# A fused graph network kernel: three pieces of the graph loaded and squared earlier, and the statistics of the sums moved behind the second kind's n term

## What is computed

```python
x = _layernorm(x + _L0_gnn_ref(x, adj, adj, gat_W, gat_a, edge_*, node_*), axis=-1)
x = _layernorm(x + _L1_gnn_ref(x, adj, adj, W_proj, b_proj, W_gcn, b_gcn), axis=-1)

# layer 0
node_support = node_adj_norm @ h
edge_output = _gru_cell(node_support, h, edge_Wih, edge_Whh, ...)
edge_support = mean over 3 heads of (softmax attention over adj * adj) @ (h @ W)
node_output = _gru_cell(edge_support, h, node_Wih, node_Whh, ...)
return de[:, None] * edge_output + dn[:, None] * node_output

# a cell
r = sigmoid(ir + hr); z = sigmoid(iz + hz); n = tanh(inn + r * hn)
return (1.0 - z) * n + z * hstate

# layer 1
filt = tanh(adj * adj) * (adj > 0)          # then the 350 largest of a row are kept
h2 = tanh(h @ W_proj + b_proj)
feat = relu(new_adj @ (h2 @ W_gcn) + b_gcn)
```

## Time and profile before

| what | value |
|---|---|
| median of 3 runs | 1315.2 us (1315.08 to 1315.21) |
| profiled execution, its own time | 1315.81 us |
| its span | 1314.5 us |
| TensorE clock granted | 0.999 of full |
| busy: PE / DVE / ACT / POOL | 1302.3 / 1015.3 / 936.2 / 100.6 us |
| transfers | 231.17 MB, 176 GB/s over the span |

### The profile page before, as it was taken

How to read it: one execution, slowest core, us unless ns; L and a number is a source line. 1 busy time by engine, 2 the same in 40 slices (tenths; PEclk the granted TensorE clock), 3 DMA queues, 4 the chain that set the end, 5 groups by cost and what they waited for, 6 DMA issues and landing times.

```text
span 1314.5 us, 12241 instructions
## 1 busy us (share of the span) xinstructions
PE 1302.3 (99%) x4197; PEld 588.7 (45%) x4197; DVE 1015.3 (77%) x1420; ACT 936.2 (71%) x968; POOL 100.6 (8%) x194
## 2 busy tenths in 40 slices
PE   9999999999999999999999999999999999999998
PEld 4444444444444444444444444444444444444445
DVE  3243333457998998999989989899857888788886
ACT  5545555348988889889889898898945556555563
POOL 0100001000100100100100100100101662000000
PEclk9999999999999999999999999999999999999999
DMA  9978888254242242242433323222114458888870
GB/s 372 414 262 274 294 296 291 84 211 145 88 146 103 97 144 96 97 144 97 149 112 108 144 96 139 102 96 96 64 34 163 146 175 290 301 289 298 294 266 18
DMA packets 45191, 231.17 MB, mean 176 GB/s; under 512 B 6530, under 2 KB 12610, under 8 KB 19778
## 3 DMA queue, kind: packets, MB, share of 16 engines
q1 hardware_dynamic: 42416, 227.50, 49.1%
q10 hardware_dynamic: 2706, 2.82, 0.6%
HBM read 226.01 MB, written 4.29 MB: 175 GB/s over the span
## 4 chain that ended last, share of the span: by engine, by line
PE 92%; DVE 5%; issue 1%; DMA 1%; ACT 1%; SPq 0%; DVEq 0%
PE t_y_ps L1888 49%; PE ns_ps L455 17%; PE t_y_ps L1438 13%; PE rows_ps L1438 4%; PE t_y_ps L1866 3%; PE t_es_ps L1855 1%; PE pos_ps L469 1%; PE t_y_ps L1403 1%; PE t_y_ps L1405 1%; DVE pieces L1249 1%; PE t_y_ps L1457 1%; ACT pieces L1166 1%; DMA mask<-in_adj_c 1%; DVE pieces L1244 1%; DVE pieces L1268 0%
## 5 line engine op out<-in xcount | busy, mean ns | idle before, releaser
L1888 PE MATMUL t_y_ps<-mask,x_sb 128*128 128x512 f32 x1536 | 662.6, 592 | 0.2 <-DVE mask L1804 0.2
L1888 PEld LDWEIGHTS t_y_ps<-mask,x_sb 128*128 128x128 f32 x1536 | 290.6, 190 | 365.3 <-issue 349.5
L1804 DVE TENSOR_TENSOR mask<-mask 128x1536 f32<-128x1536 f32 x256 | 449.4, 1756 | 0.7 <-ACT mask L1686 0.7
L1686 ACT ACTIVATE mask<-mask,ones 128x1536 f32<-128x1536 f32 x256 | 399.7, 1562 | 0.0
L1679 ACT ACTIVATE mask<-mask,pieces 128x512 f32<-128x512 f32 x352 | 241.4, 712 | 35.1 <-PE t_y_ps L1888 32.8
L1790 DVE TENSOR_SCALAR mask<-mask,e_cols 128x512 f32<-128x512 f32 x416 | 188.5, 485 | 50.1 <-PE t_y_ps L1888 44.0
L455 PE MATMUL ns_ps<-pieces,x_sb 128*128 128x512 f32 x504 | 225.1, 601 | 0.6 <-DMA x_sb<-in_x_p 0.6
L1191 ACT ACTIVATE mask<-mask 128x2048 f32<-128x2048 f32 x64 | 122.4, 1912 | 82.6 <-DVE mask L1314 82.6
L1438 PE MATMUL t_y_ps<-mask 128*128 128x512 f32 (+1 forms) x448 | 173.8, 547 | 1.5 <-DVE pieces L1249 1.5
L314 DVE TENSOR_SCALAR mask<-pieces 128x2048 fp8e4<-128x2048 f32 x64 | 77.0, 1224 | 90.1 <-DMA pieces<-in_adj_c 74.2
L1314 DVE SCALAR_TENSOR_TENSOR mask<-mask 128x2048 f32<-128x2048 f32 x64 | 143.0, 2281 | 4.3 <-DMA mask<-in_adj_c 4.3
(11 more groups left out here) (186 smaller groups left out, 575.4 us busy)
## 6 DMA issues: line engine op xcount, KB each, us to landing
mask<-in_adj_c SPq DMA_DIRECT2D x128, 1024.0 KB, 4.8
pieces<-in_adj_c SPq DMA_DIRECT2D x62, 1024.0 KB, 5.1
mask<-scratch_shifts SPq DMA_DIRECT2D x8, 1536.0 KB, 7.9
pieces<-in_adj_c SPq DMA_DIRECT2D x8, 256.0 KB, 5.0
mask<-in_x_t SPq DMA_DIRECT2D x8, 256.0 KB, 10.5
pieces<-in_x_t SPq DMA_DIRECT2D x8, 256.0 KB, 2.9
pieces<-scratch_ns_t SPq DMA_DIRECT2D x8, 256.0 KB, 4.2
mask<-in_diag SPq DMA_DIRECT2D x8, 256.0 KB, 5.6
```

Of the source, the lines that this page charges most:

```text
L1686: nc.scalar.activation(t, t, ACT.Exp, bias=ones[:, :], scale=-1.0).then_inc(exped, 1)
L1804: nc.vector.tensor_tensor(term(n), term(n), a, ALU.mult).then_inc(terms, 1)
L1888: mm = nc.tensor.matmul(y_ps[c % 2][h][:, :], x_sb[:, k, :], term(n)[:, h, :], start=k == 0, stop=k == NB - 1)
```

## The change

What it does:

- The loads of the graph's pieces 0 to 2 are issued by SP during the last chunk of attention, each as soon as the last term or shift that lay in its place has been used.
- Square and tanh of piece 0 run at the end of attention, ahead of the last `scale_y` and of the gate loop. The squares of pieces 1 and 2 are in step 0 of the gate loop, ahead of and behind `pre_n("edge")`; their tanh in steps 0 and 1.
- `measure_y` stands behind `pre_n("node")` and not ahead of it.
- SP loads x and ns for a step once the gates two steps earlier are read and x is weighed, and not once `cells` is up.
- The first graph products wait each for the one reader of their own bank.

```diff
@@ sync_tail
-        for u in range(READY):
-            load_unit(u)
         for c in range(2, NCHUNK):
+            sp.wait_ge(gates_read["node"], 3 * (c - 1))
+            sp.wait_ge(mix_step, 3 * (c - 1))
+            load_in(sp, c)
             sp.wait_ge(cells, c - 1)
-            load_in(sp, c)
             load_diag(sp, c)
-            load_unit(READY + c - 2)
+            load_unit(sp, READY + c - 2)
@@ scalar_tail
+        tanh(act, 0)
         for c in range(NCHUNK):
...
-            if c - 1 in FILTERED_IN:
-                tanh(FILTERED_IN[c - 1])
+            if c < 2:
+                tanh(act, c + 1)
             make_n("edge", c)
@@ vector_tail
         for c in range(NCHUNK):
+            if c == 0:
+                square_a(dve, 1)
             pre_n("edge", c)
+            if c == 0:
+                square_a(dve, 2)
             weigh_n("edge", c)
-            if c and c in FILTERED_IN:
-                square_a(FILTERED_IN[c])
             weigh_x(c)
+            pre_n("node", c)
             if c:
                 measure_y(c - 1)
-            pre_n("node", c)
             weigh_n("node", c)
             make_y(c)
@@ graph
-            if g == 0 and c == 0:
-                pe.wait_ge(gates_read["node"], 3 * NCHUNK)
-                pe.wait_ge(pre_step["node"], 2 * NCHUNK)
+            if g == 0 and c < len(f_ps):
+                if GATES[c] == "in_n":
+                    pe.wait_ge(pre_step["node"], 2 * NCHUNK)
+                else:
+                    pe.wait_ge(gates_read["node"], 3 * NCHUNK - 2 + READS.index(GATES[c]))
@@ sync_program
             for c in range(2):
                 load_in(sp, c)
+            sp.wait_ge(y_scaled, HEADS * (NCHUNK - 1))
+            sp.wait_ge(gaps_act, NB * (NCHUNK - 1))
+            for u in range(READY):
+                last = max((n for n in range(NPIECES) if piece_at(n) < (u + 1) * PW and u * PW < piece_at(n) + PW), default=-1)
+                if last >= 0:
+                    sp.wait_ge(terms, PIECE * (last + 1))
+                load_unit(sp, u)
@@ vector_program
+            square_a(dve, 0)
             scale_y(NCHUNK - 1)
             vector_tail(dve)
```

More of the change, by code:

```diff
@@ L985 @@
 READY = 3
-FILTERED_IN = {0: 0, 1: 1, 4: 2}
 W_SLOT, IN_SLOT = 3, 4
@@ L1077, in load_in, with load_unit, square_a, tanh @@
         sp.dma_start(ns_t[c % 2], dram["ns_t"][:, c * CW:(c + 1) * CW]).then_inc(in_loaded[c % 2], 16)
+    def load_unit(sp, u):
+        c, g = divmod(u, NPIECE)
+        sp.dma_start(piece(u).rearrange("p (k n) -> p k n", n=CW), dram["adj_c"][c, :, g * PIECE:(g + 1) * PIECE, :]
+                     ).then_inc(loaded[u % G_RING], 16)
+    def square_a(dve, u):
+        dve.wait_ge(loaded[u % G_RING], 16 * (u // G_RING + 1))
+        nc.vector.scalar_tensor_tensor(piece(u), piece(u), 0.0, piece(u), ALU.max, ALU.mult).then_inc(squared_a, 1)
+    def tanh(act, u):
+        act.wait_ge(squared_a, u + 1)
+        nc.scalar.activation(piece(u), piece(u), ACT.Tanh).then_inc(filtered, 1)
     def make_biases(dve):
@@ L1187, in make_h2 @@
             nc.scalar.activation(g_all[:, rows(c), :].rearrange("p r f -> p (r f)"), pre_h[c % 2], ACT.Tanh).then_inc(copied, 1)
-        def tanh(u):
-            act.wait_ge(squared_a, u + 1)
-            nc.scalar.activation(piece(u), piece(u), ACT.Tanh).then_inc(filtered, 1)
         def take_out(i):
@@ L1223, in scalar_tail @@
         copy_rows(end)
-        tanh(3)
+        tanh(act, 3)
         make_h2(end - 1)
         for u in range(4, NPIECE - 1):
-            tanh(u)
+            tanh(act, u)
         make_h2(end)
-        tanh(NPIECE - 1)
+        tanh(act, NPIECE - 1)
         for u in range(NPIECE, NPIECES):
-            tanh(u)
+            tanh(act, u)
             c, g = divmod(u, NPIECE)
@@ L1244, in pre_n @@
             nc.vector.scalar_tensor_tensor(hid_n[k], r[k], 1.0, hid_n[k], ALU.add, ALU.mult).then_inc(pre_step[k], 1)
-            if c == 0 and k == "edge":
-                square_a(FILTERED_IN[0])
             dve.wait_ge(pre_step[k], 2 * c + 1)
@@ L1310, in finish_x @@
             normalize(rows(c), moments, root, x_done)
-        def square_a(u):
-            dve.wait_ge(loaded[u % G_RING], 16 * (u // G_RING + 1))
-            nc.vector.scalar_tensor_tensor(piece(u), piece(u), 0.0, piece(u), ALU.max, ALU.mult).then_inc(squared_a, 1)
         def add_x1(i):
@@ L1366, in vector_tail @@
         end = NCHUNK - 1
-        square_a(3)
+        square_a(dve, 3)
         scale_h(end - 1)
-        square_a(4)
+        square_a(dve, 4)
         measure_y(end)
-        square_a(5)
-        square_a(6)
+        square_a(dve, 5)
+        square_a(dve, 6)
         scale_h(end)
-        square_a(7)
+        square_a(dve, 7)
         for u in range(NPIECE, NPIECES):
-            square_a(u)
+            square_a(dve, u)
             c, g = divmod(u, NPIECE)
@@ L1502, in tensor_tail @@
         feed(last)
-    return load_weights, load_in, load_diag, make_biases, center_weights, keep_center, sync_tail, pool_tail, scalar_tail, vector_tail, tensor_tail
+    return load_weights, load_in, load_diag, load_unit, square_a, make_biases, center_weights, keep_center, sync_tail, pool_tail, scalar_tail, vector_tail, tensor_tail
 def on_dve(k):
@@ L1587, in heads_of @@
             return slice(STRIPS * g % HEADS, STRIPS * g % HEADS + STRIPS)
-        (load_weights, load_in, load_diag, make_biases, center_weights, keep_center, sync_tail, pool_tail, scalar_tail, vector_tail,
+        (load_weights, load_in, load_diag, load_unit, square_a, make_biases, center_weights, keep_center, sync_tail, pool_tail, scalar_tail, vector_tail,
          tensor_tail) = tail_programs(
```

## The result

| | before | changed |
|---|---|---|
| median | 1315.24 us (1315.08 to 1315.8, 6 runs) | 1320.94 us (1319.67 to 1322.12, 6 runs) |
| profiled execution, its time | 1315.81 us | 1320.76 us |
| its span | 1314.5 us | 1319.4 us |
| first product of the gate loop | 978.41 | 979.09 |
| first product of the graph's piece 7 | 1104.8 (worked out in the prediction) | 1109.69 |

The ratio is 1.0042, 95% interval 1.0029 to 1.0055: slower by 5.7 us where 4.1 were forecast.

The account below looks back on a forecast made before the run. TensorE was taken as the bound, waiting about 6.5 us; the change closes a 12.9 us loop against its 11.63 us step, delaying graph piece 7 by 4.1 us: 1315.8 + 4.1 = 1319.9, median 1319.3 us, range 1313.3 to 1321.0.

Parts of the forecast that it names:

- The saved waits: TensorE's waits from attention's last product to the graph's first: removing all of them gives at most 6.5 us.
- the three waits of the earlier trace: TensorE waits 0.96 us before 991.55, 0.32 before 1005.47 and 1.46 before 1079.42; the change was to remove them.
- 5.7 forecast: Square 0 on DVE at the end of attention, ahead of the gate loop: it has 5.7 us to spare.
- the 0.32 us: TensorE's wait for a transfer before 1005.47: loading x and ns one wait earlier takes it away.
- The chain on GpSimd: GpSimd's 15 small root instructions, nine held by DVE instead of six: 8.1 us, not 6.7.
- The loop: Gate loop: statistics, GpSimd's roots, ACT's scaling and read, DVE's next statistics take 12.9 us; TensorE needs 11.63.
- The one choice that the prediction named: GpSimd's bias addition lies on DVE's L1244 by only 0.7 us; without the collision the loop is 12.4 us.
- Statistics of chunk 6: DVE's gate loop: after six turns of 12.9 us they end at 1082.9; before it was 1077.8.
- over 2 us for tanh 4 and again for tanh 7: Graph stage, a sign in the profile: TensorE waits over 2 us for each of these two tanh.
- the forecast itself: Whole kernel: a loop of 12.6 to 13.1 us gives 1317.5 to 1320.5 us, chance 0.62.
- a longer loop: Rival: ACT's or DVE's hand-overs cost 0.05 us more at each of eight; loop 13.3, 1321.7 us; 0.07 including late loads.
- +4.1 us: Graph stage: piece 7 can start at 1108.9 instead of 1104.8, and the stage moves as a whole by 4.1 us.

Follow-up runs that it names:

- The parts that give: Changed kernel with statistics ahead again and the old SP order and TensorE waits, leaving only the early loads, squares and tanh: 1310.82 us, ratio 0.9963.
- opened at ACT: Changed kernel, statistics still late, with ACT's scaling moved behind its read of r for the second kind: 1312.32 us, ratio 0.9978.
- the bias addition's collision: Changed kernel with GpSimd adding the bias to one column of each row only, the rest left out: 1316.71 us, ratio 1.0011.
- the late statistics and piece 7 ahead: Changed kernel, statistics still late, with square and tanh of piece 7 ahead of chunk 7's scaling and tanh: 1319.12 us, ratio 1.0025.
- the best version: Changed kernel with statistics ahead again, and square and tanh of piece 7 ahead of chunk 7's scaling and tanh: 1308.79 us, ratio 0.9948.
- statistics late alone: Kernel before with one edit, the statistics behind the second kind's n term; late loads and squares kept: 1326.65 us, ratio 1.008.
- four rounds: Changed kernel with four Newton rounds instead of three in GpSimd's root, 19 small instructions and not 15: 1329.04 us, ratio 1.01.
- statistics ahead: Changed kernel with only the statistics put back ahead of the second kind's n term: 1310.33 us, ratio 0.9957.
- two rounds: Changed kernel with two Newton rounds instead of three in GpSimd's root, four of 15 small instructions left out: 1309.84 us, ratio 0.9954.

## Why the prediction was right, and where it was short

**The saved waits.** As forecast: the three waits of the earlier trace rows are gone, square 0 found 5.76 us behind it (5.7 forecast), and no engine waits for the early loads. Two of the three waits go by the early pieces alone, the 0.32 us too, which the prediction had given to the loading of x and ns ("The parts that give"). Their worth I had put at 6.5 us at most; with everything else out of the way the gate loop fell from 101.01 us to 94.30, by 6.7.

**The chain on GpSimd.** It was to end 8.1 us behind the statistics, with nine members held; it ends 8.07 us behind them (1057.84 to 1065.91), with nine.

**The loop.** 12.9 us forecast, 12.93 measured. Experiments at three of its places show that it is this loop: opened at ACT it is 11.63, without the bias addition's collision 12.33 (forecast 12.4), with 11 or 19 small instructions 11.63 or 14.07. The one choice that the prediction named, whether the bias addition lies on L1248, went as forecast: 1.28 us, ending 0.54 us behind it.

**From the loop to the end.** Statistics of chunk 6 were to end at 1082.9; they end at 1083.69 in an execution whose loop starts 0.68 us later than before's, so at 1083.0 on the prediction's scale. From the loop's first product to piece 7 it was to be 4.1 us longer; it is 4.1 to 4.2 in all four profiles of the changed kernel. Where I wrote "over 2 us for tanh 4 and again for tanh 7", the rows have 2.12 and 2.05.

**What was missing.** The median of 1320.94 us lies only 0.06 us inside the upper end of the range, 1321.0, and above the 1320.5 to which the forecast itself reached; three of the six runs lie beyond 1321.0. The half microsecond between was meant for a longer loop, and the loop was not longer. So the mechanism is borne out, and that the number fell into the range was partly luck. The term "+4.1 us" was too small by 1.6 against the medians, for two causes that the table above keeps apart. First, the clock: in one of four profiled executions it fell behind the last wait, and then the time behind the first product is 5.9 us longer than before, not 4.1. The prediction counted its two waits of 2 us at their own length. A fall behind the first of them costs nothing more as long as the second wait is there: in the kernel with the small bias addition, the instructions behind the first wait took 12.23 us instead of 10.54 and the second wait shrank from 2.05 to 0.34. So, by this one profile, a fall counts behind the last wait. In the version with the late statistics and piece 7 ahead the first wait is the last, and its time behind the loop's first product (1319.22 - 978.25 = 340.97 us, with a fall) is only 0.5 to 0.7 us below that of the changed kernel without one, though a wait of 2.05 us is gone; by the medians it gained 1.8. The mean granted clock that every run's result lists bears this out: it is 0.996 to 0.998 in the five profiled executions with a fall and 0.999 in the nine without. Of the six runs of the comparison four have 0.997 or 0.998, so the clock most likely fell in those four, and two have 0.999 (1319.89 and 1320.76 us), still 4.7 and 5.5 us above the median before; but the fastest of the six, 1319.67 us, has 0.997, so the clock doesn't order them by itself. Second, the first stages: the gate loop began between 977.8 and 979.5 in all 14 profiles, whatever the kernel, and in three of the changed kernel's four it began 0.3 to 1.0 us later than before's 978.41. Twelve of the 14 have the same early loads and the same order up to there, and they alone span 977.82 to 979.45 us, so this difference arises without any in the code; executions of the kernel before differ by up to 2.2 us too. Whether the early loads add some tenths isn't shown: of kernels without them there are only two profiles (978.41 and 978.08). How the 1.6 us divide between the two causes in the six runs of the comparison stays open, since only one of them has a profile.

## What to carry to other kernels

Before moving an instruction behind another one on its engine, write down every edge that then comes back to it through other engines, and add up that loop with the durations that hold there, including those that one engine imposes on another: a loop that is 1.3 us longer than a step costs that in each step, although no engine is full. A wait removed early is worth only what the next late thing leaves of it, so follow each saved microsecond to the last engine that must wait; here the best version took the early loads and left the statistics where they were. And count a wait of TensorE of 2 us or more as possibly dearer than its length, unless another wait behind it takes up the difference.

## What was unexpected of the hardware

TensorE's granted clock fell to half (1.2 of 2.4 GHz) behind some waits of 2 to 4 us. It fell behind the waits of 4.14 us (statistics late alone) and 3.25 us (four rounds), and behind three of the twelve waits between 2.02 and 2.21 us in these profiles: 2.12 us with the small bias addition, 2.13 us with the late statistics and piece 7 ahead, 2.02 us in one execution of the changed kernel. The same wait of 2.02 us left it at 1.00 in another execution of the same program. Behind no shorter wait in the gate loop or the graph stage did it fall. A fall cost 1.5 to 1.7 us, and 2.7 behind the wait of 4.14. The four kernels without such a wait (statistics ahead, two rounds, pieces alone, and the best version) had executions within 0.7 us of each other, in four or five runs each; those with one of about 2 us spread over 1.6 to 3.8 us in six to ten. The kernel before, without such a wait, spread over 2.2 us in 13 runs, and its granted clock is 0.999 or 1.0 in all of them, so that not all of the spread is the clock's. In these runs the mean granted clock of a whole execution gives a fall away even without a profile: 1.5 to 1.7 us of 1320 are a little over a thousandth, and no run of the kernels without such a wait is below 0.999.
